# Steady phases: max and match_replace in the sigmoid's slot, the rest of the routing four to five slots up

## The reference

```python
def ffn(x, centroids, expert_biases, Ws_up, Ws_down, W_up, W_down):   # E = 64 experts, F = 64, TOP_K = 8
    xf = x.reshape(T, D)
    shared = silu(xf @ Ws_up) @ Ws_down
    aff = xf @ centroids.T
    _, idx = top_k(aff + expert_biases, TOP_K)
    w = sigmoid(take_along_axis(aff, idx, axis=1))
    w = w / (sum(w, axis=-1, keepdims=True) + 1e-08)
    cw = zeros((T, E)).at[arange(T)[:, None], idx].add(w)
    h = silu(einsum('td,edf->etf', xf, W_up))
    y = einsum('etf,efd->etd', h, W_down)
    return shared + einsum('etd,te->td', y, cw)

def attn(u, WB, WBf, w1, w2, b):
    xf = concat([u[:, :1], u[:, 1:] @ WB.T], axis=1)
    xb = concat([u[:, 1:] @ WBf.T, u[:, -1:]], axis=1)
    gamma = sigmoid(xf @ w1.T + xb @ w2.T + b)
    return gamma * (xf + xb) + (1 - gamma) * u

x = u
x = x + 0.5 * ffn(layernorm(x))
x = x + attn(layernorm(x))
x = x + 0.5 * ffn(layernorm(x))
```

## Time and profile before

| | us |
|---|---|
| median of 3 runs | 836.47 |
| lowest, highest | 836.36, 836.81 |
| span of the profiled execution | 834.9 |
| PE busy in it | 809.7 (97%) |
| DVE busy | 698.6 (84%) |
| ACT busy | 654.2 (78%) |
| POOL busy | 404.6 (48%) |

### The profile page before, as it was taken

One profiled execution on the slowest core, in us unless ns is written; L12 is line 12 of the kernel. 1 busy time (PEld: TensorE's weight loads), 2 busy tenths in 40 slices (PEclk: granted clock), 3 DMA queues, 4 the chain that ended last, 5 costly groups with the idle time before them and its releaser, 6 DMA issues.

```text
span 834.9 us, 12478 instructions
## 1 busy us (share of the span) xinstructions
PE 809.7 (97%) x3691; PEld 648.0 (78%) x3691; DVE 698.6 (84%) x1456; ACT 654.2 (78%) x1204; POOL 404.6 (48%) x355
## 2 busy tenths in 40 slices
PE   7899999999999999999999999999999999999998
PEld 5777778877778777787777877778778787788786
DVE  7998888798887988879888798787896987888875
ACT  5886679778787787877878788786878868876975
POOL 2764545544445444554545455354453644544443
PEclk9999999999999999999999999999999999999999
DMA  7000000000000000000000000000000000000000
GB/s 264 20 1 26 1 1 1 1 13 14 13 1 1 25 0 13 0 0 25 0 13 0 0 25 0 13 0 0 25 0 0 0 0 27 0 1 1 14 0 13
DMA packets 16046, 11.51 MB, mean 14 GB/s; under 512 B 1680, under 2 KB 14992, under 8 KB 16016
## 3 DMA queue, kind: packets, MB, share of 16 engines
q1 hardware_dynamic: 16016, 11.15, 4.2%
HBM read 9.05 MB, written 2.10 MB: 13 GB/s over the span
## 4 chain that ended last, share of the span: by engine, by line
PE 47%; DVE 18%; issue 15%; POOL 11%; ACT 7%; DMA 0%; POOLq 0%; DVEq 0%; ACTq 0%
POOL g_lo L351 8%; PE up L700 7%; PE up L701 7%; PE up L702 7%; PE y_ps L700 7%; PE y_ps L702 7%; PE y_ps L701 7%; DVE g_lo L578 3%; DVE up L569 3%; DVE gated L569 3%; DVE normed L515 2%; PE side L709 2%; ACT up L410 2%; ACT g_hi L418 2%; POOL rstd L341 2%
## 5 line engine op out<-in xcount | busy, mean ns | idle before, releaser
L351 POOL TENSOR_TENSOR g_lo<-gated,g_hi 128x512 fp32r<-128x512 f32 x256 | 332.3, 1298 | 370.9 <-ACT g_hi L418 370.3
L410 ACT ACTIVATE up<-up 128x512 f32<-128x512 f32 x528 | 310.9, 590 | 74.7 <-PE up L702 73.3
L569 DVE TENSOR_TENSOR gated<-up,cw 128x512 f32<-128x512 f32 x256 | 174.7, 682 | 51.6 <-ACT up L410 47.7
L569 DVE TENSOR_TENSOR up<-up,cw 128x512 f32<-128x512 f32 x256 | 175.9, 687 | 48.8 <-ACT up L410 45.5
L700 PE MATMUL up<-x_hi,wu_hi 128*128 128x512 f32 x512 | 204.3, 399 | 7.2 <-DVE g_lo L578 7.2
L700 PE MATMUL y_ps<-g_hi,wd_hi 128*128 128x512 f32 x512 | 208.4, 407 | 1.7 <-POOL g_lo L351 1.7
L702 PE MATMUL y_ps<-g_hi,wd_lo 128*128 128x512 f32 x512 | 202.4, 395 | 0.0
L701 PE MATMUL up<-x_lo,wu_hi 128*128 128x512 f32 x512 | 202.2, 395 | 0.0
L702 PE MATMUL up<-x_hi,wu_lo 128*128 128x512 f32 x512 | 201.9, 394 | 0.0
L701 PE MATMUL y_ps<-g_lo,wd_hi 128*128 128x512 f32 x512 | 201.8, 394 | 0.0
L418 ACT CAST g_hi<-gated 128x512 fp32r<-128x512 f32 x256 | 157.7, 616 | 48.1 <-DVE gated L569 45.8
(11 more groups left out here) (100 smaller groups left out, 564.1 us busy)
## 6 DMA issues: line engine op xcount, KB each, us to landing
x_in<-in_x SPq DMA_DIRECT2D x8, 256.0 KB, 2.7
wu_raw<-in_w_up SPq DMA_DIRECT2D x4, 512.0 KB, 5.8
wd_raw<-in_w_down SPq DMA_DIRECT2D x4, 512.0 KB, 6.8
x_res<-in_x SPq DMA_DIRECT2D x8, 256.0 KB, 2.7
out<-out_sb SPq DMA_DIRECT2D x7, 256.0 KB, 2.2
out<-out_sb SPq DMA_DIRECT2D x2, 128.0 KB, 1.8
sm_raw<-in_ident SPq DMA_DIRECT2D x2, 64.0 KB, 5.2
ident<-in_ident SPq DMA_DIRECT2D x1, 64.0 KB, 2.6
```

The lines of the kernel that those rows point to most:

```text
L351: nc.gpsimd.tensor_tensor(g_lo[:, i, :], gated[:, t // 2 % ORING, :], g_hi[:, i, :].bitcast(fp32), ALU.subtract).then_inc(lo_done[1], 1)
L410: nc.scalar.activation(up[i][:, :], up[i][:, :], ACT.Silu).then_inc(silu_done, 1)
L569: nc.vector.tensor_tensor(gated[:, t // 2 % ORING, :] if t % 2 else up[i][:, :], up[i][:, :], cw[ph.q][:, :], ALU.mult).then_inc(gate_done, 1)
```

## The change

In AT_STEADY_A and AT_STEADY_B the routing's entries get other slots. Nothing else changes: the same instructions run with the same operands, and the tables of the other phases stay.

```diff
--- before.py
+++ after.py
@@ -83,16 +83,16 @@
     "late": 3,
 }
 AT_STEADY_A = {
-    "x_t": 7, "x_hi": 8, "x_lo": 10, "aff": 13, "aff_sum": 14, "sig": 15, "bias": 16, "max": 18, "take": 20,
-    "gate": 22, "sum": 24, "eps": 26, "inv": 27, "cw": 28, "cw_t": 31, "cw_copy": 32,
+    "x_t": 7, "x_hi": 8, "x_lo": 10, "aff": 13, "aff_sum": 13, "sig": 15, "bias": 14, "max": 15, "take": 15,
+    "gate": 17, "sum": 20, "eps": 22, "inv": 23, "cw": 24, "cw_t": 31, "cw_copy": 32,
     "y_t": 6,
     "stat0": (12, 14), "aggr0": 16, "rstd0": 17, "norm0": (28, 30),
     "aggr2": 0, "rstd2": 1, "norm2": (2, 4),
     "y": 2, "out": 8, "keep": 11,
 }
 AT_STEADY_B = {
-    "x_t": 1, "x_hi": 2, "x_lo": 4, "aff": 8, "aff_sum": 8, "sig": 9, "bias": 10, "max": 14, "take": 15,
-    "gate": 17, "sum": 19, "eps": 20, "inv": 21, "cw": 22, "cw_t": 26, "cw_copy": 26,
+    "x_t": 1, "x_hi": 2, "x_lo": 4, "aff": 7, "aff_sum": 7, "sig": 9, "bias": 8, "max": 9, "take": 9,
+    "gate": 11, "sum": 14, "eps": 15, "inv": 17, "cw": 18, "cw_t": 26, "cw_copy": 26,
     "y_t": 6, "x1": 8, "stat1": (10, 12), "aggr1": 13, "rstd1": 14, "norm1": (16, 18), "xu": 19, "u_t": 22,
     "u_copy": 23, "attn": 28, "tanh": 29, "gamma": 30, "t1": 30, "x2": (32, 33),
     "stat2": (34, 34),
```

## The result

| | median us | lowest to highest | span of the profiled execution |
|---|---|---|---|
| before | 836.57 | 836.36 to 836.81 | 834.9 |
| after | 824.37 | 824.13 to 824.44 | 822.4 |

The ratio is 0.9853, with a 95% interval from 0.9839 to 0.9867: 12.2 us less, against 11.0 forecast. The 824.37 us lie inside the forecast range of 824 to 828, close to its lower end. The spans differ by 12.5 us.

The account below looks back on a forecast made before the run. TensorE was taken to set the pace, held up at single places. Five loop A phases (7.0 us), the A after the loop (1.0) and five B (3.0) give 11.0: 836.47 - 11.0 = 825.5 us, range 824 to 828.

Parts of the forecast that it names:

- four removable stalls: TensorE held in A before slot 21 (0.77 us), at cw_t (0.44), from A to B (0.30), in B before slot 15 (0.76).
- The room in the pause: DVE's idle time at the sigmoid covers the moved work: 2.0 of 2.66 us used in A, 2.2 of 2.73 in B.
- The margin of 0.4 us: After the pause, g_lo of tile 16 (A) and 10 (B) ends 0.4 us before TensorE wants its bank.
- the far case: In B, bias at 1.5 us and top-8 with match-replace at 1.7 overrun the pause by 0.5, said to cost nothing yet.
- the two deductions of what is late next: Losses expected on POOL's path: 0.1 us per A (rstd ahead of g_lo 17, w_sel beside), 0.15 per B (norm1 before u_t).
- the 0.44 us at cw_t: A, slot 31: TensorE's wait on POOL's w_dup, 0.44 us with slower transposes, goes as w_dup moves to slot 24.
- the 2.5 us that leave DVE's queue: Behind the sigmoid, bias (1.16 us), top-8 (0.5) and match-replace (0.8) leave the stretch where DVE had no idle time.
- The shared port (1): Rival: w_sel beside rstd and norm beside w_dup cost more, 0.4 us per A and 0.6 per B: 829.5 us, chance 0.17.
- POOL's path (2): Rival: behind the sigmoid POOL binds TensorE, both big stalls return, only cw_t and A to B won: 832.4 us, chance 0.06.
- POOL's queue in B (5): Rival: slower, as POOL waits at w_dup in slot 18 for inv, later tiles queueing behind; up to 843 us, chance 0.06.
- x_t (3): Rival: the wait of x_t in A goes as well, 6 x 0.8 us more, 820.7 us, chance 0.04.
- That each stall only moves (4): Rival: the order changes but every stall merely moves elsewhere, no change at 836.5 us, chance 0.04.

Follow-up runs that it names:

- bias_only: The kernel before with only aff, aff_sum and bias at their new slots, max, take and all behind them at the old ones: 826.50 us, ratio 0.9879.
- more_max: The changed kernel with eight more MAX8 ahead of top-8 in the five A and five B phases of the loop: 828.07 us, ratio 0.9898.
- more_max16: The changed kernel with sixteen more MAX8 ahead of top-8 in the five A and five B phases of the loop: 837.16 us, ratio 1.0007.
- to_take: The kernel before with aff, aff_sum, bias, max and take at their new slots, w_sel and all behind it at the old: 824.44 us, ratio 0.9856.

## Why the prediction was right

**The stalls and their sizes.** All four removable stalls of the earlier trace rows went, in full. A phases in the loop fell by 1.3 to 1.4 us, the one after the loop by 1.2 and B phases by 0.8 to 1.0, by the starts of their first matmuls. Forecast were 1.4, 1.0 and 0.6. Of the 0.30 us at the edge, which the forecast has in A, the 0.10 of the held matmul falls into B by these starts, so they are to be compared with 1.3 and 0.7.

**The cause.** It was put down to what stands in DVE's queue behind ScalarE's pause. The two runs without a table load show the first half (no pause, no difference between the orders), and bias_only the second (bias, with aff and aff_sum ahead of it, is worth 10.1 of 12.2 us).

**The room in the pause.** Forecast 0.5 us left in B and 0.66 in A; found 0.05 and 0.65. In B bias lasted 1.23 us and took 1.15 of the queue, where I had taken 0.7, inside its bounds. The 0.05 is less than the 0.3 to 1.2 us of idle time that I had named as a sign. Still gate 10 starts at 437.08 where its SiLU ends at 437.05, so that it cost nothing. The margin of 0.4 us behind it was right: more_max measured 0.38 in B, more_max16 0.37 in both. One sentence on it was not: in the far case, 0.5 us over, a margin of 0.4 would have left a cost of 0.1 and the held matmul, not nothing.

**The terms that were mis-sized** are the two deductions of what is late next, 0.1 in each A and 0.15 in each B, 1.25 us in all. Neither stall came, and this is the greater part of why 11.0 was 1.2 short. The A after the loop gave 0.2 more than forecast as well. In A w_sel did not get in rstd's way. DVE, and then POOL, at that place in after:

```profile
399.66 0.42 DVE L550 SCALAR_TENSOR_TENSOR w_sel<-taken,sig 128x256 f32<-128x256 f32 x1
```

```profile
399.27 0.23 POOL L339 TENSOR_SCALAR var_eps<-mv 128x4 f32<-128x4 f32 x1
399.58 1.04 POOL L341 TENSOR_TENSOR rstd<-var_eps,neg_half 128x4 f32<-128x4 f32 x1
400.59 1.30 POOL L351 TENSOR_TENSOR g_lo<-gated,g_hi 128x512 fp32r<-128x512 f32 x1
```

rstd started 0.2 us earlier within its phase than in the earlier trace rows, g_lo 17 ended at 401.89, and its matmul came at 402.26. In B the forecast was close and fell on the good side. DVE, and PE, in after:

```profile
448.05 1.92 DVE L515 TENSOR_SCALAR normed<-x,mv,rstd 128x128 f32<-128x128 f32 x2
```

```profile
450.08 0.39 PE L702 MATMUL up<-x_hi,wu_lo 128*128 128x512 f32 x1
450.31 0.60 PE L709 MATMUL side<-ident,normed 128*128 128x128 f32 x4
```

The norm beside g_lo 17 and w_dup lasted 1.92 us, where in the earlier trace rows it lasted 0.97 in B and 1.93 in A, as I had feared. It ended at 449.97, and TensorE came to u_t at 450.31 without a gap. The margin was 0.34; I had put it at 0.1 (456.1 against 456.2) and counted a small loss all the same.

**One step was right in size and wrong in its reason.** I had given the 0.44 us at cw_t to w_dup's move from slot 28 to 24. bias_only and to_take, both with w_dup in slot 28, show that the shorter backlog of DVE is enough. And the 2.5 us that leave DVE's queue are not all needed: the 1.16 of bias remove three of the four stalls but for 0.09 us at cw_t, and top-8 and match-replace the fourth, at the edge from A to B.

**Rivals.** The shared port (1) took what it was said to take from the norm in B, but no time of TensorE's. POOL's path (2) and POOL's queue in B (5) never decided: w_dup started at 448.85, directly behind g_lo 17, so inv was not waited for. x_t (3) stayed at 0.65. That each stall only moves (4) is shown wrong by the phases' lengths.

## What to carry to other kernels

When one engine has a pause that cannot be removed (here two table loads and a sigmoid, 3 us), find what its partner does in the microseconds just behind it: beyond the slack of the buffers (here 0.37 us) work there costs the bound engine one for one, and the same work ahead of the pause or inside it is free up to the pause's end plus that slack. Price such a move by the distance from the end of the pause to the release of the first buffer that is needed, not by the busy shares, which did not fall here. A wait with a name (here on w_dup) may only be a sign of the queue ahead of it, so move the head of the queue before the step that is named.

## What the runs showed of the hardware

- An elementwise VectorE instruction with two SBUF inputs (128x256, bias) took 415 to 430 ns with GpSimd idle. Started within a 128x512 subtraction on GpSimd it ended 0.27 to 0.30 us behind that one's end: 1.14 to 1.24 us in the steady phases, up to 1.53. Moving it into a time when GpSimd is idle gave back 0.77 us each, by the medians.
- The same kind of instruction did not suffer from every GpSimd instruction: w_sel, 128x256 with two SBUF inputs, took 0.42 us at 399.66 in the midst of rstd's 1.04 us (128x4, a power of two SBUF inputs). Over all sixteen of after it was 407 to 426 ns, where before one in the company of a g_lo took up to 1195. The Trainium skill's rule (SBUF — State Buffer, SBUF: two separate sides) has the two exclude each other for the whole instruction; for g_lo the trace agrees, by the common distance of the ends above, for rstd it does not. Where w_sel started 0.21 us ahead of a g_lo, w_sel kept its 0.41 us and that g_lo took 1.34 to 1.37 instead of 1.30.
- Four or eight MAX8 of 128x64 start 0.13 us apart in a row, and match-replace with its load 0.20, with 0.15 us of waiting between top-8 and the first load that needs it.
- A swap of ScalarE's table cost 1.28 us each way and nothing beside it: from 398.25 for the first load to 401.27 for the start of the next SiLU it is 3.0 us, for two loads of 1.28 and a sigmoid of 0.42.
